# Four-layer decoder on one core: integer gate and up values, a rescaled sigmoid, halved first chunks, and one output store per unit

## What is computed

```
x = x + _L1_xattn_ref(_layernorm(x, axis=-1), ctx_1024, ctx_1024, ...)
x = x + _L1_ffn_ref(_layernorm(x, axis=-1), L1_ffn_w_gate, L1_ffn_w_up, L1_ffn_w_down)
x = x + _L2_attn_ref(_layernorm(x, axis=-1), L2_attn_w_attn, L2_attn_w_proj)
```

```
def act_qdq(x):
    qmax = 2.0 ** (ACT_BITS - 1) - 1.0
    scale = jnp.maximum(jnp.max(jnp.abs(x)) / qmax, 1e-12)
    return jnp.clip(jnp.round(x / scale), -qmax - 1.0, qmax) * scale

def fixed_qdq_u16(x):
    scale = 1.0 / 65536.0
    return jnp.clip(jnp.round(x / scale), 0.0, 65535.0) * scale
...
x = act_qdq(x)
up = act_qdq(x @ lpbq_dequant(w_up).T)
gate = act_qdq(x @ lpbq_dequant(w_gate).T)
sig = fixed_qdq_u16(jax.nn.sigmoid(gate))
gate = act_qdq(gate * sig)
o = act_qdq(gate * up)
return o @ lpbq_dequant(w_down).T
```

## Time and profile before

| what | value |
|---|---|
| median of 3 runs | 1420.51 us |
| lowest and highest run | 1417.01 and 1422.38 us |
| profiled execution, first to last instruction (span) | 1418.5 us |
| median of the runs less the span | 2.0 us |
| busy share of PE, DVE, ACT over the span | 94%, 70%, 48% |
| mean granted TensorE clock | 0.975 |
| stage B in the profile | about 382.5 to 480.8 us |

### The profile page before, as it was taken

How to read it: one execution, slowest core, us unless ns; L and a number is a source line. 1 busy time by engine, 2 the same in 40 slices (tenths; PEclk the granted TensorE clock), 3 DMA queues, 4 the chain that set the end, 5 groups by cost and what they waited for, 6 DMA issues and landing times.

```text
span 1418.5 us, 42978 instructions
## 1 busy us (share of the span) xinstructions
PE 1334.8 (94%) x18644; PEld 1166.4 (82%) x18644; DVE 991.1 (70%) x2959; ACT 682.2 (48%) x1735; POOL 137.9 (10%) x299
## 2 busy tenths in 40 slices
PE   6999998999986899999999999999999999999997
PEld 6788887888643689899789889788979879989976
DVE  7957898678689554667784567796457778455767
ACT  3535763448377456333447533346632444743332
POOL 3111121111110010100110100011010010010000
PEclk9989999999997899999999999999999999999999
DMA  5000000000230200000000000000000000000001
GB/s 160 2 3 2 3 2 2 3 2 3 77 139 19 77 2 1 2 3 2 2 2 1 2 3 3 1 2 1 1 2 4 2 3 1 1 1 3 3 2 31
DMA packets 8509, 20.33 MB, mean 14 GB/s; under 512 B 2304, under 2 KB 6400, under 8 KB 7808
## 3 DMA queue, kind: packets, MB, share of 16 engines
q1 hardware_dynamic: 8320, 17.58, 3.5%
HBM read 16.53 MB, written 1.05 MB: 12 GB/s over the span
## 4 chain that ended last, share of the span: by engine, by line
PE 47%; DVE 12%; ACT 4%; issue 2%; POOL 1%; DVEq 0%
PE PS L2210 6%; PE PS L2337 6%; PE PS L1935 4%; PE PS L1967 3%; PE PS L1956 3%; PE PS L1922 3%; PE PS L2220 3%; PE PS L589 2%; PE PS L690 2%; ACT AR L1985 2%; PE PS L1947 2%; PE PS L2669 1%; PE PS L2678 1%; PE PS L1819 1%; DVE X L2740 1%
## 5 line engine op out<-in xcount | busy, mean ns | idle before, releaser
L589 PE MATMUL PS<-CC 128*128 128x128 f32 x1024 | 134.9, 279 | 0.0
L589 PEld LDWEIGHTS PS<-CC 128*128 128x128 f32 x1024 | 124.5, 193 | 3.1 <-issue 0.5
L1985 ACT ACTIVATE AR<-PS,SC 128x128 f32<-128x128 f32 x256 | 91.1, 378 | 39.3 <-DVE SC L2013 39.3
L2337 PE MATMUL PS<-AR,PA 64*64 64x256 f32 (+43 forms) x2624 | 108.6, 300 | 0.5 <-issue 0.4
L2210 PEld LDWEIGHTS PS<-AR 64*64 64x64 f32 x3072 | 100.5, 135 | 7.2 <-issue 2.2
L2210 PE MATMUL PS<-AR 64*64 64x32 f32 (+1 forms) x3072 | 103.1, 219 | 0.8 <-DVE AR L2463 0.3
L576 POOL TENSOR_SCALAR SC<-mv 128x2 f32<-128x2 f32 x64 | 13.2, 206 | 837.0 <-DVE mv L562 818.4
L2337 PEld LDWEIGHTS PS<-AR,PA 64*64 64x64 f32 x2624 | 85.0, 133 | 6.9 <-issue 2.7
L2010 DVE TENSOR_REDUCE SC<-PS 128x4 f32<-128x512 f32 x64 | 44.2, 691 | 57.1 <-PE PS L1935 56.7
L1935 PE MATMUL PS<-kvt,AR 128*128 128x128 f32 x512 | 68.8, 279 | 2.6 <-ACT AR L1980 2.6
L1935 PEld LDWEIGHTS PS<-kvt,AR 128*128 128x128 f32 x512 | 63.2, 191 | 7.9 <-ACT AR L1980 6.6
(11 more groups left out here) (552 smaller groups left out, 3334.6 us busy)
## 6 DMA issues: line engine op xcount, KB each, us to landing
WC<-in_cw SPq DMA_DIRECT2D x1, 5438.5 KB, 15.8
PA<-in_fd SPq DMA_DIRECT2D x1, 2624.0 KB, 9.3
PA<-in_stat SPq DMA_DIRECT2D x2, 1280.0 KB, 12.0
X<-in_x SPq DMA_DIRECT2D x2, 512.0 KB, 5.5
out<-X SPq DMA_DIRECT2D x1, 1024.0 KB, 5.3
CC<-in_const SPq DMA_DIRECT2D x1, 809.0 KB, 4.4
PA<-in_aw SPq DMA_DIRECT2D x1, 653.0 KB, 7.4
PA<-in_intw SPq DMA_DIRECT2D x1, 576.0 KB, 5.8
```

What stands on the lines that cost most here:

```text
L589: T.matmul(bank[int(b)][:, 0:P], lhsT=ident, rhs=CC[:, 0:P], start=True, stop=True)
L1985: A.activation(d.blocks[:, h, :], d.bank[:, h * P:(h + 1) * P], ACT.Exp, scale=D2 ** -0.5, bias=d.most[:, h:h + 1], accum_out=d.total[:, h ...
L2337: m = T.matmul(out_[:, :, first:SEQ], lhsT=FD[rows, tap:tap + 64], rhs=d.vp[rows, :, first + 1 - shift:SEQ + 1 - shift], start=starts, sto ...
```

## The change

It has seven parts. Some are a change of arithmetic, some of order.

- Gate and up are written by ACT as 32-bit integers (the conversion rounds), over the same memory. `RND` and its subtraction are dropped for them, and DVE reads the integers.
- Tanh takes the integer gate with a scale of half the gate's scale (`SCB[:, 13:14]`). The sigmoid stays in tanh's own scale: DVE clips and adds `RND / 32768 + 1` in one instruction, then subtracts `RND / 32768` and multiplies by gate in a second.
- The gate's scale is left out of the values and put into the factor of the next scale (`factor=`, `gated.factor`).
- The first chunk is handled in two halves (`FIRST`), and the first chunk of the last rounding in pieces of 128, 128 and 256 tokens (`LAST`).
- The masks and the scaling of `CN` stand ahead of the gate's chunks on DVE; the angles, the copies of the weights and the copy of the gate sums move on ACT; the gate sums and `tensor_scales` move on TensorE; the filler matmuls between products are dropped, and two instead of three stand after the third scale.
- The second half of `in_stat` goes to buffers of its own, with its DMAs right behind the first, not after `gate.sums0`.
- Each unit of stage C is stored by its own DMA once its last addition is done, ahead of the last barrier.

```
+        stat2 = [ROT[:, 1, 256 * n:256 * n + 256] for n in range(8)]
+        stat2 += [flat[:, 16384 + 256 * n:16384 + 256 * n + 256] for n in range(2)]
...
+        FIRST = ((0, 0, CH // 2), (0, CH // 2, CH))
+        WHOLE = tuple((c, 0, CH) for c in range(1, NC))
+        LAST = ((0, 0, P), (0, P, 2 * P), (0, 2 * P, CH))
...
+        def whole(ap):
+            return ap.bitcast(I32)
...
+            tensor_gate_sums(0)
             tensor_angles()
-            tensor_gate_sums(0)
+            T.wait_ge(*a.at("cross.scores.kept"))
+            tensor_scales("gated", AM[:, 12:13])
+            tensor_cross_weights("cross.out", 2, 3)
             tensor_gate_sums(1)
...
-            for c in range(NC - 1):
-                T.wait_ge(*v.at(f"product.made{c}"))
-                tensor_idle(1, 2)
             tensor_scales("product", AM[:, 12:13])
-            tensor_idle(1, 3)
+            T.wait_ge(*a.at("rotation30"))
+            tensor_idle(6, 2)
...
-            def gate_scaled(c):
-                A.activation(chunk(Gt, c), chunk(Gt, c), ACT.Identity, scale=SCB[:, 5:6], bias=cc("round")).then_inc(
-                    *a.up(f"gate.scaled{c}"))
...
+            def gate_rounded(c, lo=0, hi=CH):
+                g = chunk(Gt, c, lo, hi)
+                A.activation(whole(g), g, ACT.Identity, scale=SCB[:, 5:6]).then_inc(*a.up())
...
+                A.activation(TH[c % 2][:, :, lo:hi], whole(chunk(Gt, c, lo, hi)), ACT.Tanh, scale=SCB[:, 13:14]).then_inc(
+                    *a.up(f"tanh{c}.{lo}"))
...
             def up_rounded(c):
-                A.activation(chunk(U, c), chunk(U, c), ACT.Identity, scale=SCB[:, 4:5], bias=cc("round")).then_inc(*a.up())
-                A.wait_ge(*a.now())
-                A.activation(chunk(U, c), chunk(U, c), ACT.Identity, bias=cc("round_neg")).then_inc(*a.up(f"up{c}"))
...
+                A.activation(whole(chunk(U, c)), chunk(U, c), ACT.Identity, scale=SCB[:, 4:5]).then_inc(*a.up(f"up{c}"))
...
+            for piece in FIRST:
+                gate_rounded(*piece)
+                tanh(*piece)
+            gate_rounded(1)
             tanh(1)
+            gate_rounded(2)
             up_rounded(0)
+            tanh(2)
+            gate_rounded(3)
+            scalar_cross_weights("cross.scores", 0)
+            tanh(3)
+            up_rounded(1)
+            up_rounded(2)
+            up_rounded(3)
             scalar_angles()
...
-                V.tensor_scalar(th_, th_, 32768.0, 32768.0 + RND, ALU.mult, ALU.add).then_inc(*v.up())
-                V.wait_ge(*v.now())
-                V.tensor_scalar(th_, th_, RND, 65535.0, ALU.subtract, ALU.min).then_inc(*v.up())
-                V.wait_ge(*v.now())
-                V.scalar_tensor_tensor(g, th_, 1.0 / 65536, g, ALU.mult, ALU.mult).then_inc(*v.up(f"gated{c}"))
...
+                V.tensor_scalar(th_, th_, 32767.0 / 32768.0, RND / 32768.0 + 1.0, ALU.min, ALU.add).then_inc(*v.up())
+                V.wait_ge(*v.now())
+                V.scalar_tensor_tensor(g, th_, RND / 32768.0, whole(g), ALU.subtract, ALU.mult).then_inc(
+                    *v.up(f"gated{c}" if hi == CH else None))
...
+            vector_scales("gated", 1, 6, factor=SCB[:, 13:14])
+            V.wait_ge(*v.now())
+            V.tensor_tensor(SCB[:, 14:15], SCB[:, 7:8], SCB[:, 13:14], ALU.mult).then_inc(*v.up("gated.factor"))
...
+                V.scalar_tensor_tensor(g, whole(g), 1.0, whole(u), ALU.mult, ALU.mult).then_inc(
+                    *v.up(f"product.made{c}" if hi == CH else None))
...
+        S.dma_start(ROT[:, 1, :], stat_d[:, NSTAT // 2:NSTAT // 2 + NTOK]).then_inc(stat2_there, 16)
+        S.dma_start(flat[:, 16384:16896], stat_d[:, NSTAT // 2 + NTOK:NSTAT]).then_inc(stat2_there, 16)
         tensor_l1_ffn()
-        S.wait_ge(*main.pe.at("gate.sums0"))
-        S.dma_start(stat, stat_d[:, NSTAT // 2:NSTAT]).then_inc(stat_there, 16)
...
+        tiles_out = out.rearrange("(t p) d -> p t d", p=P)
+        for i in range(NITER):
+            for st in streams:
+                tiles = slice(TS * (NS * i + st.s), TS * (NS * i + st.s + 1))
+                S.wait_ge(*st.dve.at("L3f.x", f"c{i}"))
+                S.dma_start(tiles_out[:, tiles, :], X[:, tiles, :]).then_inc(out_written, 16)
         all_done()
-
-        S.dma_start(out.rearrange("(t p) d -> p t d", p=P), X[:, :, :]).then_inc(out_written, 16)
-        S.wait_ge(out_written, 16)
+        S.wait_ge(out_written, 16 * NITER * NS)
```

More of the change, by code:

```diff
@@ L1508, in tensor_gate_sums @@
         def tensor_gate_sums(half):
-            T.wait_ge(stat_there, 16 * (half + 1))
+            T.wait_ge(*((stat2_there, 32) if half else (stat_there, 16)))
             for n in range(10):
@@ L1512, in tensor_gate_sums @@
                 m = T.matmul(bank[2][0:80, 0:256], lhsT=cc("statsel")[:, 76 - 4 * k:156 - 4 * k],
-                             rhs=stat[:, 256 * n:256 * n + 256], start=(k == 0), stop=(k == 19))
+                             rhs=stat2[n] if half else stat[:, 256 * n:256 * n + 256], start=(k == 0), stop=(k == 19))
             m.then_inc(*main.pe.up(f"gate.sums{half}"))
@@ L1567, in tensor_l1_ffn @@
                     T.wait_ge(*a.at("rotation01"))
+                elif c == 1:
+                    T.wait_ge(*a.at("rotation11"))
                 elif c == 2:
-                    T.wait_ge(*a.at("rotation11"))
+                    T.wait_ge(*a.at("gate.sums"))
                 for t in range(CH // P):
-                    if c == 0 and t % 2 == 0:
-                        T.wait_ge(*v.at(f"product0{t // 2}"))
+                    if c == 0 and t < 3:
+                        T.wait_ge(*v.at(f"product0{t}"))
                     elif t == 0:
@@ L1647, in scalar_l1_ffn @@
             scalar_rotation(1, 1)
+            A.wait_ge(*p.at("gate.sums1"))
+            A.copy(G1S[0:80, :], bank[2][0:80, 0:256]).then_inc(*a.up("gate.sums"))
             A.wait_ge(*v.at("product.all"))
-            for c in range(NC):
-                pieces = ((0, 256), (256, 512)) if c == 0 else ((0, 512),)
-                for k, (lo, hi) in enumerate(pieces):
-                    g = Gt[:, :, c * CH + lo:c * CH + hi]
-                    A.activation(g, g, ACT.Identity, scale=SCB[:, 10:11], bias=cc("round")).then_inc(
-                        *a.up(f"product{c}{k}" if c == 0 else f"product{c}"))
+            for c, lo, hi in LAST + WHOLE:
+                g = chunk(Gt, c, lo, hi)
+                A.activation(g, g, ACT.Identity, scale=SCB[:, 10:11], bias=cc("round")).then_inc(*a.up(f"product{c}.{lo}"))
             scalar_rotation(1, 2)
@@ L1687, in vector_l1_ffn @@
             vector_scales("up", 2, 2)
[L1689 to L1706 removed]
             V.wait_ge(*v.now())
[L1708 to L1711 removed]
+            V.tensor_scalar(SCB[:, 13:14], SCB[:, 3:4], 0.5, None, ALU.mult).then_inc(*v.up("gate.half"))
             V.wait_ge(wc_there, 16)
```

103 lines of the change are left out of this document (39 added, 64 removed).

## The result

| | before | after |
|---|---|---|
| median of 9 runs | 1422.38 us | 1413.50 us |
| lowest and highest | 1417.01 and 1444.53 us | 1407.09 and 1418.62 us |
| profiled execution: time, span | -, 1418.5 us | 1418.62, 1417.3 us |
| its mean granted clock | 0.975 | 0.966 |

The ratio of the two in interleaved runs is 0.9898, with a 95% interval of [0.9864, 0.9932]; one disturbed run of before (1444.53) is left out of it. On 1420.5 us that is 14.5 us less, with an interval of 9.7 to 19.3. The kernel is faster by about 1%, where 14.3 us were forecast. The runs listed give less when they are simply averaged: the medians differ by 8.9 us, and the means without the one run (1423.7 and 1412.8) by 10.9. The forecast of 1406.2 us stood on a median of 1420.51 from three runs; the nine runs of before have 1422.38, and the median of after, 1413.50, is 7.3 above the forecast.

What follows compares the result with a forecast made beforehand. In stage B it took DVE as the bound, ACT close behind, then TensorE after the third scale. Stage B's 10.5 plus the stores' 3.8 made 14.3 us off 1418.5; with 2.0 for the runs' median, 1406.2 us, range 1400 to 1413.

Steps and rivals of the forecast that it cites:

- scales to T: Stage B, from gate and up scales ready to the third scale's factor ready (moment T): 40.5 us, 50.2 before.
- gain of stage B: Stage B ends 10.5 us earlier: 9.65 up to the third scale's factor plus 0.8 behind it; bounds 7.6 and 13.2.
- gain at the end: Kernel's end: only the last store waits for the last addition and lands in 2.4 us; 3.8 us gained, bounds 0.9 to 4.2.
- The chunks: Gate chunks on DVE and ACT: a whole chunk takes DVE 4.45 us, second maximum complete 9.3 us earlier.
- The wrong step: Second `in_stat` DMA before the gate sums: its 5.64 us wait held nothing, so moving it is worth nothing.
- Behind T: After the third scale's factor: fillers set the closing matmuls' start, low clock rises 4.9 us behind it; 0.8 us gained.
- low-clock sum of 15.6 us: TensorE's side work behind the second scale: 3.4 weight products, 7.2 sums, 5.0 rotations, done at 450.5, in time by 0.2.
- rival 2: TensorE stays at the high clock behind the third scale; stage B gains 13.2, total 1403.5 us; chance 0.13.
- rival 4: ACT's integer output is a slow path: slower than before, 1424 us, chance 0.02; milder type costs 1416, chance 0.05.
- rival 3: ACT becomes the bound in stage B and DVE's saving turns into waits; gain 10.3, 1410 us; chance 0.1.
- rival 1: Clock stays low behind the third scale for another 5.8 us; gain 11.4, 1409 us; chance 0.15.
- Rival 5: Stage C starts earlier, meets its clock changes elsewhere and gives back up to 8 us; 1414 us; chance 0.05.

Runs made afterwards that it cites:

- e3: The changed kernel with rounding in floats instead of integers for gate and up; 1418.61 us, ratio to before 0.9953.
- e11: The changed kernel with the sigmoid in three DVE instructions instead of two; 1416.44 us in its profiled run.
- e1: The kernel before with only the separate stores of stage C's units added; 1426.79 us, ratio to before 1.001.
- e10: The kernel before with only the second half of `in_stat` in buffers of its own and its DMAs early; 1435.07 us in its profiled run.
- e2: The changed kernel with the single store after the last barrier again; 1413.88 us in its profiled run.
- e5: The changed kernel without the two fillers behind the third scale; 1406.27 us at a clock of 0.976.
- e6: The changed kernel with five more fillers, three after the rotations and two at the last product; 1419.23 us in its profiled run.
- e7: The changed kernel with the old fillers, six between the products and three behind the third scale; 1420.45 us in its profiled run.

## Why the prediction was right, step by step

| step | forecast | measured |
|---|---|---|
| ACT instruction writing int32, 1536 elements; 768 | 1.57; 0.93 | 1.56; 0.93 |
| scales to second maximum | 20.9 | 20.95 |
| second scale (maximum to ACT's start); third scale (maximum to T) | 2.4; 2.3 | 2.51; 2.37 |
| scales to T | 40.5 | 40.87 |
| T to start, end of closing matmuls | 2.8, 15.95 | 2.67, 15.94 (15.31 to 15.94 in six kernels) |
| clock rises behind T at | T + 4.9 | T + 5.0 (T + 3.7 to T + 5.0) |
| gain of stage B | 10.5 | 10.1 (7.7 to 10.3, other profiles) |
| landing of the last 128 KB | 2.4 | 1.8 |
| gain at the end | 3.8 | 4.5 |
| sum | 14.3 | 14.6 in the trace, 14.5 by the ratio [9.7, 19.3], 13.9 at equal clock |

**The chunks.** The durations that the prediction took from rows for DVE and ACT held, and the layout of the two against each other told the two waits to within 0.05 us. e3 and e11 show what it rests on: the integers (7.4 us of T, on DVE and ACT alike) and the two-step sigmoid (3.9). Together that is more than the 9.3 in all: e3 pays with its longer instructions for after's order, in which all four up chunks stand ahead of the second scale, so the parts don't add up. The Trainium skill, "ScalarE: Activation LUTs", section "What ACT_TABLE_LOAD costs", gives about 93 ns for a pointer operand; the earlier trace rows agree with 1481 and 1576, 95 apart. The new instructions, with one pointer, take 1559: writing the other type costs nothing here.

**The wrong step.** "Its wait before the sums ... was before an idle TensorE and held nothing, so this is worth nothing." TensorE was idle, but ACT's copy was queued for its result, and the fourth tanh behind the copy: in that execution it held DVE for 1.0 us. The number 20.9 wasn't touched, since the new order was laid out from the scales on and not as a difference; the 9.3 us against before contains this 1.1, and against e1's stage B (29.06, T at 48.88) after gains 8.1 and 8.0. The forecast took one profile of before as the typical one. From the scales to the end of the closing matmuls it has 66.95 us, e1 and e10 have 64.48 and 65.46, and after and e2 56.81 and 56.62. So the gain of stage B is 7.7 to 10.3 us by the pairs of these profiles, and that it came out at 10.1 for 10.5 is in part the luck of this one profile.

**Behind T.** The mechanism held: fillers set the start, the clock was low at T and rose behind it. That the end agreed to 0.01 us is luck, since it is anywhere from T + 15.31 to T + 15.94 in the six kernels with this code, as the clock rises earlier or later, and that of before from T + 15.60 to T + 16.77. The 0.8 us of this term is within that spread. Two pieces were off. Without fillers the first closing matmul starts at T + 1.35 (e5), not T + 1.05. And the idle time ahead of the third maximum was not "up to 4 us": the side work ran at the high clock from 448 on and was done at 454.9, 6.4 us ahead. The prediction's low-clock sum of 15.6 us (its "nine in 3.76" is the row `444.00 3.76 PE L1529 MATMUL PS<-AR,CC 8*128 8x512 f32 x9`) would be half of that at the high clock, 8 us ahead and not 4. The price of rival 2, a high clock throughout, was 2.7 us; e6 gives 1.4 to 2.0 behind T and 0.3 ahead of it.

**The end.** The term was under by 0.7: 1.8 us in place of the 2.4 interpolated from two sizes. Its lower bound, a last store that lands late, is real: e1 (4.2) and e7 (3.2 us). In the times the stores show 2.5 (e1) and 2.9 us (e2) at equal clock, less than the 4.5.

**Rivals.** The slow path for integers (rival 4) and ACT as bound (rival 3) fall with 1.56 us. Of rival 1 nothing is seen in after: the clock rose where it did before. Rival 5, that stage C gives time back, looks true in the one profile (934.5 for 931.3), but stage C takes 927.8 to 939.9 us in the 13 profiles, with and without separate stores. Over many runs the gain is there: 14.5 us by the ratio, 13.9 at equal clock.

## What to carry to other kernels

Lay the new order of two engines out from one event with the durations of rows, and compare its absolute ends; a gain summed as differences would have missed the wait in the old order. A DMA wait before an idle engine can still hold another engine that is queued for the result, above all at the low clock. Where one profiled run is compared with another, cut them at events and set aside the stretches that weren't changed: here they hid 13 of 14 us. Then profile the old kernel more than once: its changed stretch took 66.95, 64.48 and 65.46 us in before, e1 and e10, and 2.5 us is a quarter of what was to be gained there.
